# Three orders changed in a local-attention kernel: the bias of the exponentials ahead of the query products on GpSimd, squares and copies swapped on ScalarE, one normalisation moved on VectorE

## The reference, cut to what matters

```python
def attn_layer(x, Wqkv, qs, ksc, Wo):
    q, k, v = split(x @ Wqkv)                   # 16 heads of 64
    q, k = l2norm(q) * qs, l2norm(k) * ksc
    q = q * cos * scale + rotate_half(q) * sin * scale
    k = k * cos / scale + rotate_half(k) * sin / scale
    # windows of 32 queries look at their own 32 keys and the 32 before
    attn = softmax(where(mask, -big, 8 * q @ k.T))
    return (attn @ v) @ Wo

def ffn_layer(x, g, bln, W1, b1, W2, b2):
    xn = layernorm(x) * g + bln
    a, gate = split(xn @ W1 + b1)
    return (a * gelu(gate)) @ W2 + b2

for i in range(6):
    x = attn_layer(shift_tokens(x), ...) + x
    x = ffn_layer(shift_tokens(x), ...) + x
```

## Time and profile before

| What | us |
|---|---|
| median of 3 executions | 2023.24 |
| lowest and highest | 2016.04, 2023.82 |
| profiled execution, its own time | 2016.79 |
| profiled execution, span of its instructions | 2015.0 |
| PE busy | 1808.6 (90%) |
| DVE, ACT, POOL busy | 1536.6, 1374.7, 1262.5 |

### The profile page before, as it was taken

How to read it: one execution, slowest core, us unless ns; L and a number is a source line. 1 busy time by engine, 2 the same in 40 slices (tenths; PEclk the granted TensorE clock), 3 DMA queues, 4 the chain that set the end, 5 groups by cost and what they waited for, 6 DMA issues and landing times. The chain is left out here.

```text
span 2015.0 us, 59596 instructions
## 1 busy us (share of the span) xinstructions
PE 1808.6 (90%) x24192; PEld 1005.6 (50%) x24192; DVE 1536.6 (76%) x2543; ACT 1374.7 (68%) x2862; POOL 1262.5 (63%) x1127
## 2 busy tenths in 40 slices
PE   5898898668999999999999999999999999999974
PEld 2443444534555555555555555555555555555541
DVE  4778886247887888888888888888888888887833
ACT  1454455337887777887778877788877887778832
POOL 4303200058887777878778787787877878777710
PEclk8899999768999999999999999999999999999986
DMA  9000000224433334333333333333333333323300
GB/s 191 5 2 1 2 2 2 63 48 87 97 87 74 74 74 87 81 81 72 75 86 84 79 72 77 83 89 74 72 77 83 84 79 69 70 64 78 82 1 22
DMA packets 137216, 132.63 MB, mean 66 GB/s; under 512 B 79336, under 2 KB 82984, under 8 KB 136616
## 3 DMA queue, kind: packets, MB, share of 16 engines
q1 hardware_dynamic: 136944, 128.81, 28.8%
HBM read 20.94 MB, written 1.05 MB: 11 GB/s over the span
## 5 line engine op out<-in xcount | busy, mean ns | idle before, releaser
L1013 ACT ACTIVATE prob<-s_in,lower,rq 128x64 f32<-128x64 f32 x1536 | 543.0, 431 | 37.1 <-POOL lower L1170 36.8
L866 PE MATMUL bank_a<-x_shift,wqk_sb 128*128 128x512 f32 x768 | 375.5, 612 | 13.2 <-DVE pq L1206 8.3
L885 PE MATMUL bank_y<-zT,wvo 128*128 128x512 f32 x768 | 373.2, 609 | 1.7 <-ACT zT L1009 1.7
L1141 POOL TENSOR_TENSOR prob<-prob,rden 128x1024 f32<-128x1024 f32 x96 | 182.8, 1904 | 140.0 <-DVE rden L1216 140.0
L866 PEld LDWEIGHTS bank_a<-x_shift,wqk_sb 128*128 128x128 f32 x768 | 148.2, 196 | 198.2 <-issue 190.3
L1160 POOL TENSOR_TENSOR kfin<-rk,kfin 128x512 f32<-128x512 f32 x96 | 122.2, 1273 | 150.4 <-ACT rk L1103 101.7
L885 PEld LDWEIGHTS bank_y<-zT,wvo 128*128 128x128 f32 x768 | 137.9, 190 | 153.3 <-issue 129.9
L1009 ACT ACTIVATE zT<-bank_z 128x1024 f32<-128x1024 f32 x192 | 191.9, 1012 | 22.6 <-PE bank_z L877 22.6
L383 ACT ACTIVATE a_prob<-a_sT 128x1024 f32<-128x1024 f32 x128 | 130.5, 1023 | 104.3 <-PE a_sT L217 102.4
L492 DVE TENSOR_REDUCE a_negmax<-a_max 128x1 f32<-128x512 f32 x256 | 164.6, 684 | 46.8 <-PE a_max L167 43.0
L877 PE MATMUL bank_z<-pT,xk_prev 32*128 32x128 f32 x3072 | 166.3, 286 | 9.7 <-DVE xn L1236 5.2
(11 more groups left out here) (169 smaller groups left out, 4004.2 us busy)
## 6 DMA issues: line engine op xcount, KB each, us to landing
kpad<-kfin SPq DMA_DIRECT2D x384, 128.0 KB, 2.4
qpair<-qfin SPq DMA_DIRECT2D x384, 128.0 KB, 2.4
wqk_sb<-in_wqkv SPq DMA_DIRECT2D x40, 128.0 KB, 2.6
xk_prev<-xk_own SPq DMA_DIRECT2D x24, 192.0 KB, 2.5
ffn_sb<-in_ffn SPq DMA_DIRECT2D x6, 537.5 KB, 4.4
wv_in<-in_wqkv SPq DMA_DIRECT2D x12, 256.0 KB, 4.9
wo_in<-in_wo SPq DMA_DIRECT2D x6, 512.0 KB, 6.1
xk_prev<-xk_own SPq DMA_DIRECT2D x24, 48.0 KB, 2.7
```

Source lines behind the costliest of these rows:

```text
L866: last = pe.matmul(bank_a[:, half, :], wqk_sb[:, layer_of(u) % 2, part, half, g * P:(g + 1) * P], cols(u), start=True, stop=True)
L885: last = pe.matmul(bank_y[:].rearrange("p (t w q) -> p t w q", w=WPT, q=WIN), wvo[:, layer_of(u), GH * g + 2 * (hh % 2) + hh // 2, :], zT[ ...
L1013: last = act.activation(prob[:, n % 2, i, :], s_in[:, n % 2, i, :], ACT.Exp, bias=lower[:, n % 2, i:i + 1], scale=rq[:, n % 2, i:i + 1])
L1141: pool.tensor_tensor(prob[:, e % 2], prob[:, e % 2], rden[:].unsqueeze(2).broadcast_to([P, TPB * GH, 2 * WIN]), ALU.mult).then_inc(pn_ok, 1)
```

## The change

It adds no arithmetic and removes none. Three lists are put in another order.

- GpSimd, every step: `lower` (L1170) now stands before the two `qfin` instructions, and `sumq` stays behind them.
- ScalarE, three kinds of step with the ordinary list: the second square of the queries (L1115) moves behind the first copy z23, and `xnT` behind six exponentials. In the LINEAR step: the second table change moves ahead of the second square of the keys; the first square of the queries moves behind the inverse norm of the queries, the second one behind both copies; ten instead of nine exponentials stand ahead of the keys' inverse norm, and the sixteenth moves to the front of the next step.
- VectorE: `xn` moves from before the mask additions to behind the bound of the key sums (`floor_ok`). The blocks of ADD, SUM, OUTPUT and LINEAR are written in another order.

```diff
@@ ScalarE, top of every step
+                if quarter(e) and unit_at(s - 1, LINEAR) is not None:
+                    exponentials(e, 15, TPB * GH).then_inc(exp_ok, 1)
@@ ScalarE, LINEAR step
                         act.activation(sq[:, 0, :], bank_a[:, 0, :], ACT.Square).then_inc(sqk0_ok, 1)
+                    act.preload_act_table_set("natural_log_exp_and_others")
+                    if quarter(n):
                         after(act, pk2_ok, n)
                         act.activation(sq[:, 1, :], bank_a[:, 1, :], ACT.Square).then_inc(sqk_ok, 1)
-                    act.preload_act_table_set("natural_log_exp_and_others")
...
-                        exponentials(d, 0, 9)
+                        exponentials(d, 0, 10)
...
-                        after(act, q_mm, n)
-                        after(act, sumk_ok, n)
-                        act.activation(sq[:, 0, :], bank_a[:, 0, :], ACT.Square).then_inc(sqq0_ok, 1)
+                    if quarter(d):
+                        exponentials(d, 10, 11)
...
                     if quarter(n):
-                        after(act, pq2_ok, n)
-                        act.activation(sq[:, 1, :], bank_a[:, 1, :], ACT.Square).then_inc(sqq_ok, 1)
-                    if quarter(d):
-                        exponentials(d, 9, 11)
+                        after(act, q_mm, n)
+                        after(act, sumk_ok, n)
+                        act.activation(sq[:, 0, :], bank_a[:, 0, :], ACT.Square).then_inc(sqq0_ok, 1)
...
                         copy(z[:, 0:2, :], bank_z[:, 0:2, :]).then_inc(z01_ok, 1)
+                    if quarter(n):
+                        after(act, pq2_ok, n)
+                        act.activation(sq[:, 1, :], bank_a[:, 1, :], ACT.Square).then_inc(sqq_ok, 1)
                     if quarter(d):
-                        exponentials(d, 11, 16).then_inc(exp_ok, 1)
+                        exponentials(d, 11, 15)
@@ ScalarE, other steps
+                    if quarter(d):
+                        exponentials(d, 6, 12)
                     u_turned = unit_at(c, NORM)
...
                         act.activation(xnT[:], bank_z[:, 3, :], ACT.Identity, ...).then_inc(xnT_ok, 1)
-                    if quarter(d):
-                        exponentials(d, 6, 12)
...
-                    if quarter(n):
-                        after(act, pq2_ok, n)
-                        act.activation(sq[:, 1, :], bank_a[:, 1, :], ACT.Square).then_inc(sqq_ok, 1)
                     if quarter(e):
...
                         copy(z[:, 2:4, :], bank_z[:, 2:4, :]).then_inc(z23_ok, 1)
+                    if quarter(n):
+                        after(act, pq2_ok, n)
+                        act.activation(sq[:, 1, :], bank_a[:, 1, :], ACT.Square).then_inc(sqq_ok, 1)
@@ GpSimd
-                    after(pool, pq_ok, n)
-                    after(pool, qpair_in, n - 1, 64)
-                    pool.tensor_tensor(qfin[:, 0, :], pq[:, 0, :], pq[:, 1, :], ALU.subtract).then_inc(qfin0_ok, 1)
-                    pool.tensor_tensor(qfin[:, 1, :], pq[:, 2, :], pq[:, 3, :], ALU.add).then_inc(qfin_ok, 1)
                 if quarter(c):
                     after(pool, max_ok, c)
                     after(pool, rq_ok, c)
                     after(pool, exp_ok, c - 2)
                     pool.tensor_tensor(lower[:, c % 2], s_max[:], rq[:, c % 2], ALU.mult).then_inc(lower_ok, 1)
                 if quarter(n):
+                    after(pool, pq_ok, n)
+                    after(pool, qpair_in, n - 1, 64)
+                    pool.tensor_tensor(qfin[:, 0, :], pq[:, 0, :], pq[:, 1, :], ALU.subtract).then_inc(qfin0_ok, 1)
+                    pool.tensor_tensor(qfin[:, 1, :], pq[:, 2, :], pq[:, 3, :], ALU.add).then_inc(qfin_ok, 1)
                     after(pool, sqq_ok, n)
@@ VectorE
-                if u_back is not None:
-                    ...  # xn
                 if quarter(c):
                     ...  # s_in
                     dve.tensor_scalar(rk[:], bank_f[:], 1e-24, None, ALU.max).then_inc(floor_ok, 1)
+                if u_back is not None:
+                    ...  # xn
+                if quarter(n):
                     after(dve, q_mm, n)
...
+                if u_add is not None:
+                    ...
                 if u_sum is not None:
...
-                if u_add is not None:
-                    ...
+                if u_out is not None:
+                    ...
                 if u_lin is not None:
...
-                if u_out is not None:
-                    ...
```

More of the change, by code:

```diff
@@ L1231, in step @@
                                   prob[:, e % 2].rearrange("p h (k n) -> p h k n", n=WIN)).then_inc(pT_ok, 1)
-                if u_back is not None:
-                    after(dve, rstd_ok, u_back)
-                    after(dve, xnT_mm, u_back - 1)
-                    for t in range(TPB):
-                        last = dve.tensor_scalar(xn[:, t, :], bank_z[:, 2, t * P:(t + 1) * P], mv[:, t, 0:1],
-                                                 rstd[:, t:t + 1], ALU.subtract, ALU.mult)
-                    last.then_inc(xn_ok, 1)
                 if quarter(c):
@@ L1249, in step @@
                     dve.tensor_scalar(rk[:], bank_f[:], 1e-24, None, ALU.max).then_inc(floor_ok, 1)
+                if u_back is not None:
+                    after(dve, rstd_ok, u_back)
+                    after(dve, xnT_mm, u_back - 1)
+                    for t in range(TPB):
+                        last = dve.tensor_scalar(xn[:, t, :], bank_z[:, 2, t * P:(t + 1) * P], mv[:, t, 0:1],
+                                                 rstd[:, t:t + 1], ALU.subtract, ALU.mult)
+                    last.then_inc(xn_ok, 1)
+                if quarter(n):
                     after(dve, q_mm, n)
@@ L1258, in step @@
                     dve.tensor_reduce(s_max[:], s_in[:, c % 2], AX.X, ALU.max, negate=True).then_inc(max_ok, 1)
+                if u_add is not None:
+                    after(dve, y_mm, 4 * u_add + 3)
+                    lo, hi = cols(u_add, 0, 64), cols(u_add, 64, P, 1)
+                    dve.tensor_tensor(lo, bank_y[0:64, :], lo, ALU.add)
+                    dve.tensor_tensor(hi, bank_y[64:P, :], hi, ALU.add).then_inc(xa_ok, 1)
                 if u_sum is not None:
@@ L1268, in step @@
                     last.then_inc(mv_ok, 1)
-                if u_add is not None:
-                    after(dve, y_mm, 4 * u_add + 3)
-                    lo, hi = cols(u_add, 0, 64), cols(u_add, 64, P, 1)
-                    dve.tensor_tensor(lo, bank_y[0:64, :], lo, ALU.add)
-                    dve.tensor_tensor(hi, bank_y[64:P, :], hi, ALU.add).then_inc(xa_ok, 1)
+                if u_out is not None:
+                    after(dve, ff_mm, u_out)
+                    lo, hi = cols(u_out, 0, 64), cols(u_out, 64, P, 1)
+                    dve.scalar_tensor_tensor(lo, bank_z[0:64, 3, :], ff_column(u_out, 2 * FCH)[0:64], lo, ALU.add, ALU.add)
+                    dve.scalar_tensor_tensor(hi, bank_z[64:P, 3, :], ff_column(u_out, 2 * FCH)[64:P], hi, ALU.add,
+                                             ALU.add).then_inc(xf_ok, 1)
                 if u_lin is not None:
@@ L1280, in step @@
                     last.then_inc(hid_ok, 1)
-                if u_out is not None:
-                    after(dve, ff_mm, u_out)
-                    lo, hi = cols(u_out, 0, 64), cols(u_out, 64, P, 1)
-                    dve.scalar_tensor_tensor(lo, bank_z[0:64, 3, :], ff_column(u_out, 2 * FCH)[0:64], lo, ALU.add, ALU.add)
-                    dve.scalar_tensor_tensor(hi, bank_z[64:P, 3, :], ff_column(u_out, 2 * FCH)[64:P], hi, ALU.add,
-                                             ALU.add).then_inc(xf_ok, 1)
             dve.memset(kpad[:].rearrange("p a n -> p (a n)"), 0.0).then_inc(kpad_zero, 1)
```

## The result

The changed kernel takes 2045.6 us (median of 4 runs, 2039.2 to 2052.1) beside 2020.8 us of the kernel before on the same chip: the ratio is 1.013, with a 95% interval of 1.0098 to 1.0162. It is slower, by about 25 us, where 12 were forecast. In the experiments, five executions of 2551 to 9596 us (one of e5, one of e6, three of the kernel before) are left out of the ratios.

The account below looks back on a forecast made before the run. PE, busy 90% of the span, plus its holes bound the kernel. Units +6.7 (21 at +0.32), start-up +7.9, cover -2.4: +12.2 us, so 2029 profiled; adding the median's 6.4 gives 2035, range 2014 to 2046.

Parts of the forecast that it names:

- GpSimd waits for `s_max` in each step: `lower` waits 1.2 us in the NORM step, making `sumq` and the GATE step's key sum late: +0.59 us a unit.
- ScalarE +0.29, -0.56: GATE into LINEAR: second key square later behind the table change, +0.29 us; LINEAR into OUTPUT: copy z23 earlier, -0.56 us.
- VectorE's other blocks cost nothing: ADD, LINEAR, SUM and OUTPUT blocks keep their old order inside each pair, so nothing moves: 0 us.
- the earlier bound pays: Rival: no POOL wait for `s_max` in the NORM step; NORM-to-GATE step 13.7, 21 us faster, 2002; chance 0.13.
- the wait for `xn` that the prediction put at nothing: NORM step: PE weighs its rows some 0.35 us later because of `xn_ok`, ending before the key sum: no cost.
- Start-up steps of 14.6 us: Start-up steps take 14.6 us in place of 13.52 through the late `qfin` and `sumq`; nine steps together +7.9 us.
- One has a hole of 1.5 us of PE's own that covers it, 0: One of the nine start-up steps has its own PE hole, so the late `sumq` costs 0 there.
- In about four units PE has a longer hole of its own at the GATE step's scores, which covers the 0.59: -2.4: GATE step's scores: PE's own longer hole hides the 0.59 us delay in about four units, -2.4 us in all.
- the third rival: More than counted, 2046: late `qpair` DMAs delay GATE scores, or wider start-up holes keep the clock low (+11); chance 0.12.

Follow-up runs that it names:

- e5: Kernel before, with SP starting two more copies of `qfin` behind the four `qpair` copies of each step; 2018.3 us beside 2017.5, ratio 1.0005.
- e6: Changed kernel with `s_max` ahead of the query products on VectorE; 2021.7 us beside 2017.5 of the kernel before, ratio 1.0021.
- e1: Kernel before with GpSimd's new order alone (`lower` ahead of both `qfin`); 2048.6 us beside 2015.8, ratio 1.0157.
- e4: Kernel before with VectorE's part of the change alone (`xn` behind the key bound); 2006.1 us beside 2015.8, ratio 0.9950.
- e2: Changed kernel with GpSimd's old order (both `qfin` ahead of `lower`); 2005.7 us beside 2015.8 of the kernel before, ratio 0.9944.

## Where the prediction held and where it failed

The direction was right, the size was not: +24.7 us beside the kernel before where +12.2 were forecast. The time of 2045.6 lies 10 above the forecast, at the very end of the range; the base of 2023.2, the median of three, was itself 2.4 above the 2020.8 of four.

- *GpSimd waits for `s_max` in each step.* Right: 1.20 us in the NORM step, N-G 14.78 for a forecast +0.59. e1 shows it alone (14.76).
- *ScalarE +0.29, -0.56.* Right: +0.34 and -0.55. A unit: +0.40 for a forecast +0.32, at 19 units some +7.5 us.
- *VectorE's other blocks cost nothing.* Right as far as the steps show, but the part by itself gains (e4). The rival "the earlier bound pays" had the right sign for these two parts together: e2 is 10 us faster, of its 21. Its step of 13.7 did not come, N-G took 14.14, because the wait for `xn` that the prediction put at nothing costs PE 6.5 us in L877 over the 1385 us of the grouped lines. GpSimd's order is what kept this rival from deciding.
- *Start-up steps of 14.6 us.* Right for each regular one (14.62), wrong in the sum. The first three of the nine steps lost 1.2 us (forecast 3.3), the one with the hole 1.6 (0), the next three 4.5 (3.2), the last two 6.7 (1.4): 14.1 in place of 7.9. "One has a hole of 1.5 us of PE's own that covers it, 0" was wrong: that step took 16.60 instead of 14.96 us, its hole did not cover the delay, it grew with it. The last two hold a new hole of 3.23 us and 6.8 us at 1.2 GHz behind it. At 660 us the changed kernel was only 9.9 us further behind than at the start of the part, close to 7.9 by luck: its first step happened to be 1.2 us shorter, and between 563 and 660 us it won 3 back, because the kernel before had a hole at 627 us and 3.4 us at 1.2 GHz behind it that the changed one had not.
- *"In about four units PE has a longer hole of its own at the GATE step's scores, which covers the 0.59: -2.4".* This is the step that failed. I took those holes for a fixed length of PE's own, under which a delay of the data disappears. They are instruction blocks arriving late, and their end moves with the data. Of the four, two came again in the same steps and did not shrink (1.67 us of idle time became 2.51, 1.98 became 2.15), two did not come, and eleven came in other steps. In place of -2.4 stand +13.3 us (22.0 less 8.7).
- *The granted clock.* The sum had no term for it from the start-up on; the third rival had it for five start-up steps. The runs show 13.7 us more at 1.2 GHz between 520 and 1905 us, which at half the speed is up to 6.9 us.

The terms as measured: 9.9 up to 660 us, some 7.5 in the typical length of the 19 units that follow, and 14.5 by which single long steps are longer than before (23.3 against 8.8 over the typical step): 31.9 of the 32.2 us between the two profiles. The 14.5 hold 11.2 of the 13.3 us of holes, and the clock, with 10.3 us more at 1.2 GHz in this stretch (17.1 against 6.8), up to 5.1 us; the rest of both lies in the 9.9 or behind the last of these units.

The third rival, at 2046, met the time, and both of its ways point at something that happened, though neither as it stood. It named the late `qpair` copies: three scores of the start-up are released by a `qpair` DMA (2.1 us together, 0.6 before), and none later; what the late copies brought with them is late blocks. It named the clock for five steps of the start-up; the clock fell in single stretches behind long holes, in the regular part too. With +13.3 in place of -2.4 the forecast's own sum is 27.9 us, beside 32.2 between the two profiles, from which the 13.3 come, and 24.7 between the medians.

## What to carry to other kernels

A hole that the profile puts down to nothing but "issue" is no cover: ask what sets its end, and whether that end moves with the change. Then look at the granted clock in the window of the step behind it, not in 40 slices of the whole: here a step behind a long hole took 1.7 us more. In a dense run of small matmuls look whether the holes stand a fixed number of instructions apart; if they do, late blocks of instructions are the first thing to think of. That the last operand should be in place well before the run, not at its start, is what e2 and e6 suggest; no run moved it by itself to an earlier time. And before an instruction is put ahead of another on an in-order queue, see whether its input comes later than the other's: here 0.2 us of work with a late input held back four copies and two sums, in every step.

## What the runs showed of the hardware

- TensorE's instructions came in packets of 16 KB on a queue of their own, one for each 256 recorded instructions (194, 195 and 196 packets for 0, 255 and 511 records more). All 145 holes of over 0.3 us inside the scores, in fourteen kernels, stand exactly at a border between two such blocks.
- A product of 32-bit floats takes two loads and two products of the record: 32 of them moved every hole to another step.
- A late block makes a gap of up to 3.5 us from start to start in the changed kernel (3.45), and of 4.4 in e4 (4.38), where the 128 products around it take 1.48 us together.
- Behind a hole of 2.51 us the granted clock was 0.50 (1.2 GHz) for 3.4 us, and the step there took 17.29 us in place of 15.59 with PE busy for 16.93; behind one of 1.67 us it stayed at 1.00.
- ACT's load of a table took 1.28 us and the next activation started 0.01 us behind it, whether that was a Gelu, an exponential or a square.
